# Second-layer attention of tile 0, and norm and projections of tile 1, moved inside the last FFN chunk

## The reference

```python
x = x + L0_xattn(layernorm(x), ctx)   # 32 heads of 128, 8 kv heads, with biases
x = x + L0_ffn(layernorm(x))          # below
x = x + L1_xattn(layernorm(x), ctx)   # rmsnorm inside, 32 heads of 16, 8 kv heads
x = x + L1_ffn(layernorm(x))          # top 2 of 8 experts, mean of relu(x @ W_e + b_e)

def L0_ffn(h):
    logits = h @ gate_w; routing, _ = top_k(logits, 2)
    shared = relu(h @ up_w) ** 2 @ down_w
    routed = ((h @ fc1_w) @ expert_w * sum(routing)) @ fc2_w
    return layernorm(shared + routed) * gamma + beta
```

## Time and profile before

| | |
|---|---|
| median of 3 runs | 1921.33 us |
| profiled execution | 1922.17 us |
| its span in the trace | 1920.4 us |
| TensorE busy, matmuls | 1795.8 us, 94% |
| VectorE busy | 1234.7 us, 64% |
| ScalarE busy | 901.6 us, 47% |
| GpSimd busy | 493.8 us, 26% |

### The profile page before, as it was taken

How to read it: one execution, slowest core, us unless ns; L and a number is a source line. 1 busy time by engine, 2 the same in 40 slices (tenths; PEclk the granted TensorE clock), 3 DMA queues, 4 the chain that set the end, 5 groups by cost and what they waited for, 6 DMA issues and landing times. The chain is left out here.

```text
span 1920.4 us, 36262 instructions
## 1 busy us (share of the span) xinstructions
PE 1795.8 (94%) x14128; PEld 988.5 (51%) x14128; DVE 1234.7 (64%) x2288; ACT 901.6 (47%) x1433; POOL 493.8 (26%) x367
## 2 busy tenths in 40 slices
PE   5879999999999999999999999985999999899997
PEld 2545555555555555555555444443555555555553
DVE  5765655655555556556465677766677777777863
ACT  5544344443434343444434332325666666666662
POOL 0051641605207044075000000000223222323323
PEclk9899999999999999999999999996999999999999
DMA  5011220401204012035100300030000000000000
GB/s 225 23 45 45 78 100 2 143 1 67 78 1 144 1 46 99 1 110 187 57 1 28 133 1 1 0 132 1 7 7 6 13 7 6 8 12 6 7 12 12
DMA packets 18378, 88.82 MB, mean 46 GB/s; under 512 B 2608, under 2 KB 2864, under 8 KB 10160
## 3 DMA queue, kind: packets, MB, share of 16 engines
q1 hardware_dynamic: 18224, 86.58, 12.4%
HBM read 65.60 MB, written 20.97 MB: 45 GB/s over the span
## 5 line engine op out<-in xcount | busy, mean ns | idle before, releaser
L599 PE MATMUL bank<-R 128*128 128x512 f16 (+1 forms) x7152 | 1311.2, 343 | 35.6 <-DVE R L1371 14.0
L599 PEld LDWEIGHTS bank<-R 128*128 128x128 f16 x7152 | 586.6, 99 | 681.1 <-issue 48.3
L1371 DVE SCALAR_TENSOR_TENSOR R<-bank,biases,R 128x512 f16<-128x512 f32 x288 | 204.4, 745 | 264.8 <-ACT R L1012 223.9
L450 POOL TENSOR_TENSOR R<-R 128x512 f32<-128x512 f32 x112 | 157.1, 1402 | 452.9 <-ACT R L1211 451.7
L1012 ACT ACTIVATE R<-bank,biases 128x512 f16<-128x512 f32 x128 | 87.4, 686 | 252.6 <-PE bank L599 251.9
L346 POOL TENSOR_SCALAR R<-R 128x2048 f32<-128x2048 f32 (+1 forms) x20 | 33.7, 1686 | 440.5 <-PE bank L599 378.9
L1211 ACT ACTIVATE R<-R,msk 128x512 f32<-128x512 f32 x128 | 90.3, 716 | 60.2 <-DVE R L1699 60.2
L1456 DVE SCALAR_TENSOR_TENSOR X<-bank,X 128x512 f32<-128x512 f32 x128 | 86.7, 682 | 35.5 <-PE bank L599 35.4
L1383 DVE SCALAR_TENSOR_TENSOR R<-bank,R 64x512 f16<-64x512 f32 x64 | 44.0, 688 | 101.2 <-ACT R L1020 100.8
L1699 DVE SCALAR_TENSOR_TENSOR R<-bank,R 128x512 f32<-128x512 f32 x128 | 86.9, 679 | 30.4 <-PE bank L599 29.5
L599 PE MATMUL bank<-CT,R 128*128 128x512 f16 x384 | 90.6, 387 | 11.7 <-DVE CT L1345 11.7
(11 more groups left out here) (145 smaller groups left out, 2089.6 us busy)
## 6 DMA issues: line engine op xcount, KB each, us to landing
R<-in_wB SPq DMA_DIRECT2D x16, 1024.0 KB, 5.8
R<-in_wX SPq DMA_DIRECT2D x16, 1024.0 KB, 4.9
w_split<-AW SPq DMA_DIRECT2D x16, 1024.0 KB, 4.8
R<-w_split SPq DMA_DIRECT2D x12, 1024.0 KB, 7.3
R<-in_ctxT SPq DMA_DIRECT2D x4, 1024.0 KB, 10.1
X<-in_x SPq DMA_DIRECT2D x4, 1024.0 KB, 13.8
out<-X SPq DMA_DIRECT2D x16, 256.0 KB, 2.0
R<-in_wB SPq DMA_DIRECT2D x7, 512.0 KB, 5.7
```

The costliest lines, as they stand in the source:

```text
L450: g.tensor_tensor(acc, acc, tmp[:, e % 2, :], ALU.add).then_inc(e_acc, 1)
L599: last = pe.matmul(dst, a(sa), b(sb_), start=(k == 0), stop=(k == m - 1))
L1371: v.scalar_tensor_tensor(out=dst, in0=src, scalar=bias, in1=hi, op0=ALU.add, op1=ALU.subtract).then_inc(done, 1)
```

## The change

- `Place` is a table of buffers and banks. Tiles 1 to 15 keep theirs (`REST`). Tile 0 gets others (`TILE0`), in the region `R1` (which holds an expert's weights later) and in `R3`, and uses banks 1, 2, 3, 4, 6 and 7 at times when the chunk does not.
- The last chunk is a function of its own on each compute engine, `ffn_last`. Its twelve jobs, four down and four fc2 products keep their order, and all of step 0, the norms of tiles 0, 1 and 2, and `project`, `turn_q` and `turn_k` of tile 1 stand between them. The second layer's loop starts with step 1.
- On the DMA queue (SyncE), the experts' biases (`be`) and the weights of experts 0 and 1 are loaded later, since their places are in use.
- On GpSimd two memsets for tile 0's padding come earlier, in places of their own.
- In the first layer's steps 0 to 2, ScalarE and VectorE read `proj(0)` before the second half's probabilities and `proj(1)` before the context split; until now both came behind these.

```diff
+        TILE0 = Place(qs=heads(R1[:, 1024:3072]), PT=R1[:, 1024:3072], ks=kheads(R1[:, 3072:4096]), qT=qturned(R1[:, 4096:6144]),
+                      ... E=exps(R3[:, 0:1024]), ..., b_q=2, b_kv=3, b_tq=(6, 7), b_tk=4, b_s=(2, 3), b_tp=((6, 7), (0, 1)), b_pv=4, b_to=1, b_y=4)
 # SyncE
-            expert(0)
-            expert(1)
             sp.wait_ge(u_mm, 12 * NC)
             expert(4)
             expert(5)
+            sp.wait_ge(b_o, 2)
+            expert(0)
+            sp.wait_ge(a_y, 1)
+            sp.dma_start(R3, be.broadcast_to([P, NE * D])).then_inc(be_in, 16)
+            sp.wait_ge(n_lo, ffn_stat(0) + 1)
+            expert(1)
             sp.wait_ge(f_mm, 2 * NT)
 # TensorE
+            def ffn_last(c):
+                ffn_job(c, 0)
+                ffn_job(c, 1)
+                ffn_job(c, 2)
+                tile_turn(pe, attn_turn(0), 0, 4, attn_turn(0))
+                ffn_job(c, 3)
+                ...
+                project(0, ctx_tile(0), T20)
+                ffn_job(c, 4)
+                ffn_job(c, 5)
+                turn_q(0)
+                ffn_job(c, 6)
+                turn_k(0)
+                ffn_job(c, 7)
+                scores(0, 0)
+                ffn_job(c, 8)
+                ffn_job(c, 9)
+                scores(0, 1)
+                ffn_job(c, 10)
+                turn_p(0, 0)
+                ffn_job(c, 11)
+                weigh_v(0, 0)
+                ffn_down(c, 0)
+                ffn_fc2(0)
+                turn_p(0, 1)
+                ffn_down(c, 1)
+                weigh_v(0, 1)
+                ffn_fc2(1)
+                tile_turn(pe, attn_turn(1), 1, 5, attn_turn(1))
+                ffn_down(c, 2)
+                turn_o(0)
+                ffn_fc2(2)
+                output(0)
+                project(1, ctx_tile(1), T2[0])
+                ffn_down(c, 3)
+                ffn_fc2(3)
+                turn_q(1)
+                turn_k(1)
 # ScalarE, first layer, steps 0 to 2
                 exp(0)
                 exp(1)
+                if early:
+                    proj(0)
                 phi(0)
                 phi(1)
+                if early:
+                    proj(1)
                     ... (context hi)
 # ScalarE, last chunk
+            def ffn_last(c):
+                norm_root(act, attn_stat(0), 0)
+                job(c, 0)
+                y_root(c * TC - 1)
+                job(c, 1)
+                tile_hi(act, attn_stat(0), 0, TILE0.yn)
+                job(c, 2)
+                tile_store(act, attn_turn(0), 4, ...)
+                job(c, 3)
+                project_hi(0)
+                ...
+                job(c, 11)
+                exponentials(0, 1)
+                out_hi(0, 0)
+                y_root(c * TC)
+                turned_p(0, 1)
+                norm_root(act, attn_stat(1), 1)
+                ...
 # VectorE, first layer, steps 0 to 2: prob(0), proj(0), prob(1), plo(0), plo(1), proj(1), context lo, stats
 # VectorE, last chunk
+            def ffn_last(c):
+                norm_stats(dve, attn_stat(0), 0, x_tile(0), True)
+                job(c, 0)
+                norm_apply(dve, attn_stat(0), 0, x_tile(0), TILE0.yn)
+                y_stats(c * TC - 1)
+                job(c, 1)
+                tile_lo(dve, attn_stat(0), 0, TILE0.yn)
+                job(c, 2)
+                job(c, 3)
+                y_norm(c * TC - 1)
+                job(c, 4)
+                q_lo(0)
+                kv_lo(0)
+                y_add_to_x(c * TC - 1)
+                job(c, 5)
+                ...
+                job(c, 7)
+                less_max(0, 0)
+                job(c, 8)
+                gate_sums(c)
+                job(c, 9)
+                row_sums(0, 0)
+                reciprocals(0, 0)
+                probs_lo(0, 0)
+                job(c, 10)
+                less_max(0, 1)
+                job(c, 11)
+                ... (rest of tile 0 and the norms of tiles 1 and 2, between the y of the chunk's tiles)
+                y_of(c, 3)
+                y_stats(NT - 1)
+                y_norm(NT - 1)
+                y_add_to_x(NT - 1)
```

More of the change, by code:

```diff
@@ L16 @@
+from collections import namedtuple
 from contextlib import ExitStack
@@ L802, in ffn_chunk @@
-                    group3(banks[bf], [(lambda p, k=k: eoT[:, p, k, tt], lambda p, k=k: Wfc2[:, p, k, :])
-                                       for k in range(2)], f_mm)
-                    n = c * TC + NT + TC
-                    if last and t == 0:
-                        tile_turn(pe, 32, 0, 4, 32)
-                    elif not last and t < 2:
+                    ffn_down(c, t)
+                    ffn_fc2(t)
+                    if t < 2:
                         for u in (2 * t, 2 * t + 1):
@@ L922, in attn_step @@
                     expert(n - 1, 0, T2[1 - buf])
-                if more and not n_is_first(n):
+                if more:
                     pe.wait_ge(r_lg, n)
@@ L1183, in ffn_chunk @@
-                for t in range(TC):
-                    if t == 0 and not last:
-                        store(0)
-                        tile_hi(act, n + 2, 0, rel[:, 0, :])
-                    if t < TC - 1:
-                        y_root(c * TC + t)
-                    if t == 0 and not last:
-                        store(1)
-                        tile_hi(act, n + 3, 1, rel[:, 1, :])
-                    if t == 1 and not last:
-                        store(2)
-                        store(3)
@@ L1202, in norm_store @@
+                store(3)
+                y_root(c * TC + 2)
             def norm_store(n, buf):
@@ L1497, in b_step @@
                 prob(0)
-                add_last(0)
+                if isinstance(s, int) and s < NC - 1:
+                    proj(0)
+                else:
+                    add_last(0)
                 prob(1)
@@ L1502, in b_step @@
                 plo(1)
-                proj(0)
+                if not (isinstance(s, int) and s < NC - 1):
+                    proj(0)
                 add_last(2)
@@ L1510, in b_step @@
                 stats()
-                proj(1)
+                if not (isinstance(s, int) and s < NC - 1):
+                    proj(1)
                 proj(2)
@@ L1591, in ffn_chunk @@
+            def ffn_chunk(c):
                 first = isinstance(c, int) and c == 0
-                for q, (kind, m) in enumerate(JOBS):
+                for q in range(12):
                     if q in (1, 4, 5) and not first:
                         {1: y_stats, 4: y_norm, 5: y_add_to_x}[q](c * TC - 1)
-                    if 7 <= q < 11 and not last:
+                    if 7 <= q < 11:
                         v.bn_stats(cbn[:, q - 7, :], x_tile(c * TC + TC + (q - 7))).then_inc(n_bn, 1)
@@ L1657, in ffn_chunk @@
                     y_stats(n)
-                    if t == 0 and not last:
+                    if t == 0:
                         xlo(2)
@@ L1761, in attn_step @@
                 less_max(n, 0)
[L1762 to L1763 removed]
                 if two:
                     expert(n - 2, 5)
[L1766 removed]
+                if two:
                     ffn_lo(n - 1)
@@ L1827, in _ @@
+            ffn_chunk(0)
+            with dve.Fori(1, NC - 1) as c:
+                ffn_chunk(c)
+            ffn_last(NC - 1)
             attn_step(1)
```

509 lines of the change are left out of this document (296 added, 213 removed).

## The result

The changed kernel takes 1905.85 us, median of four runs (1901.55 to 1907.36); the kernel before, run beside it, 1921.25 (1919.45 to 1921.79). The ratio is 0.9917, with a 95% interval of 0.9902 to 0.9933: 15.4 us faster. The forecast was 1907.5, in a range from 1897 to 1918. The profiled execution of after took 1907.36 us, 1905.6 of it span, so this pair of profiles explains 14.8 us.

The account below looks back on a forecast made before the run. TensorE, busy 94%, was held up by VectorE's readings in the first layer; VectorE's work limited the last chunk. Gains of 10.5 + 3.3 = 13.8 us gave 1908.4 profiled, median 1907.5, range 1897 to 1918.

Parts of the forecast that it names:

- part 1: First layer's steps 0 to 2: reading projections 0 and 1 earlier gains 10.5 us, bounds 5 to 15.6.
- step 0: First layer: gain at `proj(2)` 2.9 + 2.5, but `proj(4)` waits about 2.7; 1.5 us taken, bounds 0 and 3.
- step 1: First layer: same new wait, and VectorE perhaps held by GpSimd; 3 us gained, bounds 1 and 6.
- step 2: First layer, no statistics: wait of 4.06 and nearly all of 2.55 slow clock gained; 6.0 us, bounds 4 to 6.6.
- GpSimd in step 1: First layer: if VectorE's small operations fall under GpSimd's first instruction, the step gains 1 us instead of 3.
- The walk through the chunk: Last chunk followed in written order: 79 us of VectorE work plus some 20 of waits; step 1's first maximum at 1329.
- Part 2: Last chunk with second layer's step 0 inside: 3.3 us gained, bounds -5 to 13.
- Edits at nothing: Later bias and expert weight loads, earlier GpSimd memsets and the unchanged loop from step 2 on: no effect on time.
- A: Last chunk hides more: idle brings no low clock, VectorE waits 11; 12 us gained there, total 22.5, 1899; chance 0.20.
- B: Little from the first layer: it gives 6, the last chunk between 3 and -3; 1912 to 1918 us; chance 0.18.
- C: No gain: four more slow groups in the chunk and ScalarE queueing once more; net 0, 1921 us; chance 0.05.
- D: Slower: TensorE stays at 1.2 GHz through the chunk's job phase, thirteen slow groups; 1931 us; chance 0.05.

Follow-up runs that it names:

- part 1 alone: The kernel before with only the earlier reading of projections 0 and 1 in the first layer's steps 0 to 2; 1910.71 us, ratio 0.9951.
- job 3 first: The changed kernel with tile 0's transpose on TensorE and its store on ScalarE behind job 3 instead of ahead; 1902.49 us, ratio 0.9913.
- root first: The changed kernel with ScalarE taking tile 1's root and the second turned probabilities ahead of y 0's root; 1904.01 us, ratio 0.9910.
- more TensorE: The changed kernel with 24 extra matmuls ahead of the second and third tiles' fc2 products in the last chunk; 1903.03 us, ratio 0.9907.
- more VectorE: The changed kernel with six extra unread statistics operations on VectorE between the last chunk's y tiles; 1907.76 us, ratio 0.9932.
- chunk reordered: The changed kernel with "job 3 first" and "root first" together, and tile 0's turned probabilities behind job 11; 1900.28 us, ratio 0.9888.
- filled idle: The changed kernel with 24 unread matmuls in TensorE's idle time ahead of tile 0's transpose in the last chunk; 1896.25 us, ratio 0.9879.
- projection 2 first: The changed kernel with VectorE reading projection 2 ahead of the statistics in the first layer's steps 0 to 2; 1910.38 us, ratio 0.9936.
- GpSimd later: The changed kernel with GpSimd's weight split of the first layer's step 1 held until that step's projections are read; 1900.52 us, ratio 0.9897.
- readers first: "GpSimd later" with statistics and norm behind all projection and output readers in steps 0 to 2, outputs 0 and 1 before transposes; 1905.46 us, ratio 0.9913.
- both of these: The changed kernel with the edits of "chunk reordered" and "readers first" together; 1895.49 us, ratio 0.9873.
- part 2 alone: The changed kernel with the old order in the first layer's steps 0 to 2, so only the last chunk's change; 1916.83 us, ratio 0.9978.

## Why the prediction was right, point by point

- **The bound.** Right. In the chunk VectorE's work sets the time: 3.9 us more of VectorE cost 3.4, 5.2 us more of TensorE cost 1.3. In the first layer its readings do, together with GpSimd, which holds VectorE up.
- **`proj(2)`, steps 0 to 2.** Right: no wait in any of them, 2.75 long in step 0. The new wait before `proj(4)`, said to be 2.7 in steps 0 and 1, measured 2.61 and 2.71.
- **The terms of part 1.** 10.5 was forecast and 9.1 is in this profile, but the terms were off singly. TensorE's long runs of matmuls at the end of each step say how they split. Timeline of TensorE, before and after:

```profile
85.40 9.33 PE L599 MATMUL bank<-R 128*128 128x512 f16 x84
...
131.34 9.33 PE L599 MATMUL bank<-R 128*128 128x512 f16 x84
```

```profile
82.71 11.92 PE L642 MATMUL bank<-R 128*128 128x512 f16 x96
...
125.02 11.92 PE L642 MATMUL bank<-R 128*128 128x512 f16 x96
```

 The table gives what each step gained over before, counted from the start of step 0's scores to these runs and to S3. The seven kernels have the first-layer order of after unchanged: part 1 alone, job 3 first, root first, more TensorE, more VectorE, chunk reordered, filled idle.

| us gained | step 0 | step 1 | step 2 | sum |
|---|---|---|---|---|
| forecast | 1.5 | 3 | 6.0 | 10.5 |
| after | 2.7 | 3.6 | 2.8 | 9.1 |
| the seven kernels | 1.2 to 3.3 | 2.3 to 3.4 | 5.3 | 8.9 to 11.1 |
| projection 2 first | 0.6 | 1.0 | 6.2 | 7.7 |
| GpSimd later | 3.3 | 8.0 | 4.5 | 15.8 |

 Step 0 was put too low and step 2 too high. Step 2's term took the gain of its wait and its slow group whole and did not ask what comes next on VectorE there. The reader of projection 0 now stands between the halves of the probabilities, whose lo halves can fall beside GpSimd's additions. Timeline of VectorE, then of GpSimd, kernel after:

```profile
134.76 1.38 DVE L1555 SCALAR_TENSOR_TENSOR AW<-AW,smx 128x512 f32<-128x512 f32 x1
136.06 3.43 DVE L1560 TENSOR_TENSOR AW<-AW 128x512 f16<-128x512 f32 x2
```

```profile
127.71 11.23 POOL L429 TENSOR_TENSOR X<-X,R 128x512 f32<-128x512 f32 x8
```

 That GpSimd is the cause, the other kernels settle, though none was made for it. One lo half takes 0.68 when GpSimd does not run and 1.75 beside an addition. In the kernel after both lie beside additions: 3.43, waits of 0.93 and 1.06 before the transposes, a slow group of 4.32, and 2.8 gained. In each of the seven kernels the additions end before the second: 2.36, one wait of about 1.03, the group at 2.76, and 5.3 gained. In "projection 2 first" both come behind the additions, as they do in the kernel before (additions over at 140.31, lo halves 1.47 from 140.78): no wait, and 6.2 gained, which is the forecast of 6.0. With "GpSimd later" GpSimd is busy there with its split: 3.94, waits of 0.90 and 0.94, and 4.5 gained. So the term holds where GpSimd stays clear, and the 2.8 of this profile is its lowest value in any kernel. Whether the slow group follows the two waits is open: of the four kernels that have them ("readers first" and "both of these" are the others), only the kernel after shows it.
- **GpSimd in step 1.** A hold was there again, of 1.77 on 4 columns, beside a GpSimd instruction of 1.90 (timeline of VectorE, then of GpSimd, kernel after):

```profile
103.33 1.77 DVE L527 TENSOR_TENSOR cstat<-cstat 128x4 f32<-128x4 f32 x1
```

```profile
103.20 1.90 POOL L396 TENSOR_SCALAR R<-R 128x2048 f32<-128x2048 f32 x1 [50.36 <-DMA R<-in_wB]
```

 By the Trainium skill, SBUF — State Buffer, section "Who interferes with whom", a VectorE instruction with two SBUF inputs contends with a GpSimd instruction that reads SBUF, and whoever issues first has the shared port pair for the whole instruction; the ends that coincide in three kernels agree. The operation held here, and the one of 1.10 us in the earlier trace rows, is a TENSOR_TENSOR of that kind, not an instruction in the two-port mode that the prediction named; in "projection 2 first" a TENSOR_SCALAR on the same 4 columns was held too, for 1.87. The consequence of the hold was forecast as "step 1 gains 1 instead of 3" if the small operations fall under GpSimd's first instruction. One did, and step 1 still gained 3.6: only the last of them was caught, for 1.77, and three had passed. The 3 that the sum used was near what the eight kernels with this order show, 2.3 to 3.6; the 1 was too low. What GpSimd costs in this step is more than one small operation: the two norm operations behind it took 2.58 in after and 1.00 with "GpSimd later", and step 1 gained 8.0 there.
- **The walk through the chunk** held at the stations that it named. Idle before tile 0's transpose 5.6 forecast, 5.44 measured; VectorE's waits 5.9 and 3.8, measured 6.20 and 3.84; job 3 slow, 5.25; idle before the turned probabilities 3.9, measured 3.58; the wait for tile 1's root 2.8, measured 2.66; VectorE without a pause 35 us, measured 34.3.
- **Part 2's term**, 3.3, was 4.1 with part 2 alone and 5.5 in this profile. What separates the last two is the group behind the wait of 3.58, counted as slow: it was slow in seven kernels, at 4.44 each, and at full clock in the kernel after and in "filled idle"; in "job 3 first" the slow time fell on the transposes and the group together. No run says which it will be.
- **Edits at nothing.** The transfers were rightly put at nothing: from 1230 us on, no engine of the kernel after waits for a DMA. The loop was not: the stretch behind M, which holds its turns, took back 1.5 us.
- **Luck.** The waits of both stretches were named rightly, but that the sum came so near is partly luck. Against the profile, step 2 was 3.2 too high and the loop 1.5, while steps 0 and 1 and part 2 were 1.2, 0.6 and 2.2 too low, and 1.7 came between S3 and Y, where nothing was changed.
- **Rivals.** A needed short waits without the low clock: job 3 and `proj(4)` were slow, though the second group in the chunk was not, and A's 12 us in the chunk came only in "both of these" (12.4). B forecast 6 from part 1: the kernels with this order show 8.9 to 11.1. C and D needed four or more further slow groups in the chunk: there was one slow group in after, and two in most others.

## What to carry to other kernels

Where the order is written by hand, walk the queue of the engine that holds TensorE up, instruction by instruction with measured durations; that found the five waits of the chunk that it named to 0.3 us. A reader moved forward pays only if nothing else of the same engine stands between it and the next reader that is waited for; moved within the same work it shifts the wait. And look at what GpSimd does beside VectorE's operations, the small ones too: one wait that kept it away gained 4.4 to 5.3 us, more than the whole rebuilt chunk alone (3.6).

## What the runs showed of the hardware

- VectorE's operations on 4 columns take 0.15 to 0.17 us, and 1.68 to 1.90 when caught beside a GpSimd operation on SBUF of 1.90; they end within 0.02 us of it.
- The lo half of the probabilities, two inputs of 128x512 f32, takes 0.68 us on VectorE alone and 1.75 beside a GpSimd addition of 128x512.
- TensorE behind a wait of 2.6 to 2.7 us took either 2.76 or 4.13 to 4.45 us for twelve matmuls of 128x512, and behind 3.58 either 2.75 or 4.44, in kernels with the same instructions there. With matmuls that nobody reads in the idle time, the group behind took 2.75 instead of 5.25, and the stretch was 2.9 us shorter.
- "Issue" waits at the two turns of the second layer's loop were 2.2 to 3.4 us in all kernels but the two with 24 more matmuls ahead of the loop, "more TensorE" (0.29 and 0.16) and "filled idle" (none). From M to the end these two took 583.3 and 580.8 us, against 589.6 after and 586.5 at least in the others; how much of that is the turns is not measured. I suspect where the loop's instructions come to lie, but no run changed only that, so it stays open. The gains in the medians of these two kernels hold this effect too, and only their M - Y speaks for the chunk.
- Not tried: "GpSimd later" together with the chunk's reordering and the fill, which by these rows act on different stretches.
